# Semaphores of an eight-layer kernel cleared at two seams of six, stores waited for one stage later, and two attention openings reordered

## The chip, the cores and the metric

The kernel runs as one program on 1 core of a Trainium2 chip. Five engines work side by side, each through its own queue in order: TensorE (PE; its weight loads are listed as PEld), VectorE (DVE), ScalarE (ACT), GpSimd (POOL) and SyncE (SP, which here only issues transfers and waits). They meet through semaphores. The metric is the device time of one execution in microseconds, lower is better. The kernel before was timed in three runs: median 1087.17 us, lowest 1084.04, highest 1089.96.

## The reference

x has 2 batches of 1024 tokens of width 256 (2048 rows, 16 tiles of 128 rows); the context has 77 tokens for each batch. Four layer pairs are added to x in turn, each on a layer-normed copy:

```
x = x + attn0(ln(x), ctx, mask)      # 16 heads of 16, biases bq bk bv bo
x = x + ffn0(ln(x))                  # 8 experts, the two best, softmax gates
x = x + attn1(ln(x), ctx, mask)      # 16 heads of 16, bias bo only
x = x + ffn1(ln(x))                  # int8-rounded product with a 256x256 matrix
x = x + attn2(ln(x), ctx, mask)      # one head, context as keys and values
x = x + ffn2(ln(x))                  # 8 experts, two of them in groups, silu
x = x + attn3(ln(x), ctx)            # 16 heads of 64, rotary, relative position bias
x = x + ffn3(ln(x))                  # 8 experts of capacity 320, an overflow path

attn: softmax((q Wq + bq)(k Wk + bk)^T / sqrt(16), masked) (v Wv + bv) Wo + bo
ln:   (x - mean) / sqrt(var + 1e-5)
```

## The kernel before

x stays on chip as 16 tiles. The program is a row of seven stages, in this order: the load stage (`load_stage`), attention 0 (`attn16` with n = 0), the first experts (`moe0`), attention 1 (`attn16` with n = 1), the middle stage (`middle`: ffn1, attn2 and ffn2), the fourth attention (`attn_gqa`), and the last experts (`moe3`).

**Seams.** `run_stage` (L113) runs one stage. Each stage is one block of instructions per engine, and a block ends with a barrier: every engine drains, POOL collects them and releases all. These instructions carry the line of the stage's `with nc.Block()` (L181, L329, L729, L997, L1860). Behind it `run_stage` clears and frees the stage's semaphores (L120, a drain and one range clear on POOL) and sets a second barrier (L121). This is done after every stage but the last, six times.

**The stages' semaphores.** `sem` (L101) allocates one and puts it on the stage's list. By the code the lists have 14 in the load stage, 31 in each `attn16`, 30 in `moe0`, 85 in `middle` and 28 in `attn_gqa`. Semaphores that outlive a stage are allocated in `build` (L2690 to L2706) and never cleared.

**moe0 and the bias stores.** Beside the experts' products (L867, TensorE, and L779 and L782, VectorE) the stage prepares the position bias of the fourth attention: ScalarE loads it by tiles, POOL adds the mask (L852), and ScalarE issues 16 stores, one for each tile, 616 KB each, to DRAM (L829), the last when the last tile is nearly done. The stores count on two semaphores, `masked_out`. SyncE issues the loads of attention 1, the masks and nine large fills of DRAM, and at its end waits until all 16 stores have landed (L750). The fourth attention, two stages on, reads them back.

**The opening of attn16.** Ahead of the loop over 16 tiles:
- TensorE: keys (L489) and values (L495) of the context; then `value_blocks` (L504), 20 records of 128x128 that spread the values over blocks, which waits for VectorE's copy of V (`v_raw`); then for tile 0 `lnT`, two transposes of the normalised rows (L513), and `queries` (L520); then `lnT` of tile 1; then the loop, whose first step is the scores (L529, L535).
- VectorE: mean and variance of all 16 tiles (L146 to L154), the wait for TensorE's values and V's copy with its bias (L369, or L372 without), then the wait for ScalarE's square root and the reciprocal (L374), the masked keys (L378, which TensorE awaits ahead of the scores), the masked copies of the value blocks (L388, six), and in the loop the row maximum (L396), the shift (L402), sum (L414) and reciprocal (L417).
- POOL: the wait for the reciprocal, three tiles of normalisation (L336), three output biases (L341), and in the loop the scaling of the probabilities (L345).
- ScalarE: the square root (L166), two copies of the keys (L427), the copy of the transposed rows (L435) and of the queries (L442, or L445 without bias), and in the loop the exponentials (L457).

The value blocks use banks 4 to 6 of PSUM, the transposes and queries bank 7, the scores banks 0 to 3.

Of the kernel before, what the change touches and what calls it, by code (L numbers as in the profile page):

```python
# [19 lines left out]
NT = T // P  # L20
# [80 lines left out]
def sem(c, name):  # L101

    c.stage_sems.append(c.nc.alloc_semaphore(name=name))
    return c.stage_sems[-1]
# [5 lines left out]
        c.nc.tensor.matmul(bank[:, :], c.identb[:, :], c.RQ[:, :, :].rearrange("p k n -> p (k n)"), start=True, stop=True)  # L110


def run_stage(c, stage, last=False):  # L113


    with ExitStack() as c.stage_ctx:
        c.stage_sems = []
        stage()
    if not last:
        c.nc.clear_and_free_semaphores(c.stage_sems)  # L120
        c.nc.all_engine_barrier()  # L121


def xt(c, i):
# [176 lines left out]
def attn16(c, n, has_bias, scale, n_in):  # L301


    nc = c.nc
# [22 lines left out]
    heads = lambda ap: ap.rearrange("p (h k) -> p h k", k=SK)  # L327

    with nc.Block() as block:  # L329
        @block.gpsimd  # L330
        def _(pool):
            pool.wait_ge(rstd_ok, 1)

            def layer_norm(i, b):
                wait(pool, lnT_ps, i - 1)
                nc.gpsimd.tensor_scalar(c.ln[b][:, :], xt(c, i), mean_of(c, i), rstd_of(c, i),  # L336
                                        ALU.subtract, ALU.mult).then_inc(ln_ok, 1)

            def output_bias(i):
                pool.wait_ge(ln_ok, i + 1)  # L340
                nc.gpsimd.tensor_tensor(xt(c, i), xt(c, i), c.bo[:, :], ALU.add).then_inc(biased, 1)  # L341

            def normalise(i, b):
                pool.wait_ge(rd_ok, i + 1)
                nc.gpsimd.tensor_tensor(heads(c.prob[b]), heads(c.prob[b]),  # L345
                                        rden[b][:, :].unsqueeze(2).to_broadcast([P, H, SK]),
                                        ALU.mult).then_inc(norm_ok, 1)
            layer_norm(0, 0)
            layer_norm(1, 1)
            layer_norm(2, 0)  # L350
            pool.wait_ge(w_in, 16 * n_in)
            for i in range(3):
                output_bias(i)
            for t in range(NT):
                normalise(t, t % 2)
                if inside(t + 4 - 1):
                    layer_norm(t + 3, (t + 3) % 2)
                    output_bias(t + 3)

        @block.vector  # L360
        def _(dve):
            chain = Chain(dve, chain_s)
            nv = nc.vector
            dve_variance(c, chain, ve_ok)
            dve.wait_ge(w_in, 16 * n_in)
            dve.wait_ge(v_ps, 1)
            src = bank_v[0:SK, :].rearrange("k (b n) -> k b n", b=B)
            if has_bias:
                nv.tensor_tensor(V[:, :, :], src, c.bv[0:SK, :].unsqueeze(1).to_broadcast([SK, B, D]),  # L369
                                 ALU.add).then_inc(v_raw, 1)  # L370
            else:
                nv.tensor_copy(V[:, :, :], src).then_inc(v_raw, 1)  # L372
            dve.wait_ge(std_ok, 1)
            nv.reciprocal(c.rstd[:, :], c.std[:, :]).then_inc(rstd_ok, 1)  # L374
            dve.wait_ge(k_sb, 2)
            for k in range(KC):
                for b in range(B):
                    last = nv.tensor_tensor(KB[:, k, b, :, :],  # L378
                                            KT[:, k, b * SK:(b + 1) * SK].unsqueeze(1).to_broadcast([P, HPR, SK]),
                                            c.hmask[:, :].unsqueeze(2).to_broadcast([P, HPR, SK]), ALU.mult)  # L380
            last.then_inc(kb_ok, 1)
            for q in range(3):
                dve.wait_ge(vb_ps, q + 1)
                j0, j1 = q * VPART, min((q + 1) * VPART, NBLK)
                src = bank_vb[q][:, 0:(j1 - j0) * B * VHEADS * HD].rearrange("p (j b g e) -> p j b g e", b=B, g=VHEADS, e=HD)
                sel = vsel[:, j0 * VHEADS:j1 * VHEADS].rearrange("p (j g) -> p j g", g=VHEADS)
                for b in range(B):
                    last = nv.tensor_tensor(VB[:, b, j0:j1, :].rearrange("p j (g e) -> p j g e", e=HD), src[:, :, b],  # L388
                                            sel.unsqueeze(3).to_broadcast([P, j1 - j0, VHEADS, HD]), ALU.mult)
                last.then_inc(v_sb, 1)  # L390

            def step(t, b):

                if inside(t):
                    dve.wait_ge(s_ps, t + 1)
                    nv.reduce_max(c.mx[:, :].rearrange("p (r h) -> p r h", r=GROUPS),  # L396
                                  sview.rearrange("p r (h k) -> p r h k", k=SK), AX).then_inc(mx_ok, 1)
                    wait(dve, pT_ps, (t - 1) * PG)
                    dve.wait_ge(mx_ok, t + 1)
                    for u, done in ((0, shiftA), (1, shiftB)):  # L400
                        r = slice(2 * u, 2 * u + 2)
                        nv.tensor_tensor(c.prob[b].rearrange("p (r h k) -> p r h k", r=GROUPS, k=SK)[:, r],  # L402
                                         sview[:, r].rearrange("p r (h k) -> p r h k", k=SK),
                                         c.mx[:, :].rearrange("p (r h) -> p r h", r=GROUPS)[:, r].unsqueeze(3)
                                         .to_broadcast([P, 2, HPB4, SK]), ALU.subtract).then_inc(done, 1)
                if inside(t - 2):
                    dve.wait_ge(y_ps, t - 1)
                    dve.wait_ge(biased, t - 1)
                    nv.tensor_tensor(xt(c, t - 2), xt(c, t - 2), bank_y[:, 0:D], ALU.add).then_inc(y_used, 1)
                    dve.wait_ge(y_used, t - 1)  # L410
                    nv.bn_stats(bst_of(c, t - 2), xt(c, t - 2))
                if inside(t):
                    dve.wait_ge(exp_ok, t * 2 + 2)
                    nv.reduce_sum(c.den[:, :], heads(c.prob[b]), AX).then_inc(den_ok, 1)  # L414
                    dve.wait_ge(den_ok, t + 1)
                    wait(dve, norm_ok, t - 1)
                    nv.reciprocal(rden[b][:, :], c.den[:, :]).then_inc(rd_ok, 1)  # L417
            pipeline(dve, step, 0, 4, NT - 2, NT + 2)
# [64 lines left out]
        def _(pe):  # L483
# [15 lines left out]
            def value_blocks():  # L499

                pe.wait_ge(v_raw, 1)
                for j, h0 in enumerate(VHEAD0):
                    key0, o = j * P % SK, j % VPART * B * VHEADS * HD
                    last = nt.matmul(bank_vb[j // VPART][:, o:o + B * VHEADS * HD], c.tiled_f[:, key0:key0 + P],  # L504
                                     V[:, :, h0 * HD:(h0 + VHEADS) * HD], start=True, stop=True)
                    if j % VPART == VPART - 1 or j == NBLK - 1:
                        last.then_inc(vb_ps, 1)
# [60 lines left out]
                                     start=(k == 0), stop=(k == KC - 1))  # L568
                last.then_inc(y_ps, 1)

            value_blocks()
            lnT(0, 0)
            queries(0, 0)
            lnT(1, 1)
            pe.wait_ge(kb_ok, 1)

# [134 lines left out]
def moe0(c, d):  # L711

    nc = c.nc
# [8 lines left out]
    rel = [sb(c, f"m0_rel{j}", [P, HB, SK]) for j in range(2)]  # L722
    masked = [sb(c, f"m0_masked{j}", [P, HB, SK]) for j in range(2)]
    rel_in = [sem(c, f"m0_rel_in{j}") for j in range(2)]
    masked_out = [sem(c, f"m0_masked_out{j}") for j in range(2)]
    row_in, row_ok, masked_ok = sem(c, "m0_row_in"), sem(c, "m0_row_ok"), sem(c, "m0_masked_ok")
    gates = g8(c.gates)
    mraw2 = c.prob_pair[1][0:SK, 0:B * S].bitcast(I32)
    with nc.Block() as block:  # L729
        @block.sync  # L730
        def _(sp):
# [14 lines left out]
            for j in range(8):  # L746
                sp.dma_start(c.xd2[j * part * P:(j + 1) * part * P, :].rearrange("(p r) n -> p r n", r=part),
                             c.hole[:, :].unsqueeze(1).to_broadcast([P, part, XW])).then_inc(c.holes, 16)
            for b in range(2):
                sp.wait_ge(masked_out[b], 16 * (NT // 2))  # L750

        @block.vector
        def _(dve):
# [1913 lines left out]
def build(nc, d):  # L2667
    c = Core()
    with ExitStack() as ctx:
# [34 lines left out]
        c.maskT2 = sb(c, "maskT2", [SK, B * S], BF16)  # L2704
        c.hole = sb(c, "hole", [P, XW])
        c.holes = nc.alloc_semaphore(name="holes")  # L2706
        c.xd2 = nc.dram_tensor("routed_rows", (XROWS, XW), F32, kind="Internal").ap()
        c.yd2 = nc.dram_tensor("routed_results", (2 * T, D), F32, kind="Internal").ap()
        c.mb_dram = nc.dram_tensor("masked_bias", (NT * P, H * SK), F32, kind="Internal").ap()
# [15 lines left out]
        c.psall_t = ctx.enter_context(nc.psum_tensor("psum", [P, 8 * 512], F32))  # L2725
        c.psall = c.psall_t[:, :]
        c.ps = [c.psall[:, k * 512:(k + 1) * 512] for k in range(8)]
        run_stage(c, lambda: load_stage(c, d))
        run_stage(c, lambda: attn16(c, 0, True, HD ** -0.5, N_ATTN0))
        run_stage(c, lambda: moe0(c, d))  # L2730
        run_stage(c, lambda: attn16(c, 1, False, HD ** -0.5, N_ATTN0 + N_ATTN1))
        with ExitStack() as both:
            c.stage_ctx = both
            gqa_tiles(c)
            run_stage(c, lambda: middle(c, d))
            run_stage(c, lambda: attn_gqa(c, d))
        run_stage(c, lambda: moe3(c, d), True)


def host_arrays(inputs):  # L2740
# [81 lines left out]
```

## Time and profile before

| what | value |
|---|---|
| three runs, median (lowest to highest) | 1087.17 us (1084.04 to 1089.96) |
| the profiled execution | 1097.08 us, span 1095.2 us, 17120 instructions |
| TensorE busy | 900.1 us, 82% |
| VectorE busy | 742.6 us, 68% |
| ScalarE busy | 374.7 us, 34% |
| POOL busy | 383.3 us, 35% |
| mean granted TensorE clock | 0.919 |

The span reaches from the first to the last instruction, the profiled execution's time also holds what lies around it. Busy shares are averages over seven stages with different limits. In the views below a time is in us from the span's start; a name like POOLq or PEldq is an engine's instruction queue, where barriers, semaphore waits and drains run, which don't count as busy. In brackets stands how long an engine stood idle ahead of an instruction and what ended it. PEclk is the granted clock of TensorE as a share of full speed.

### The profile page before, as it was taken

What the parts mean: (1) busy time and instruction counts of PE and PEld (TensorE: products, weight loads), DVE (VectorE), ACT (ScalarE), POOL (GpSimd) and SP (SyncE); (2) the same over time, 40 slices, a digit from 0 to 9 for tenths busy, and PEclk for the clock granted to TensorE, in tenths of its full rate; (3) what the DMA queues carried; (4) which work ended last, traced back from release to release, by engine and by line L of the source; (5) the groups of instructions that cost most, each with busy time, mean ns of one, the idle gap of its engine ahead of it and who ended that gap; (6) DMA issues with size and microseconds to landing.
All of it is one profiled execution on the core that took longest, in us unless ns stands there. A gap on an engine that the chain in (4) does not pass through costs nothing. (4 is left out here: it accounts for less than half of the span.)

```text
span 1095.2 us, 17120 instructions
## 1 busy us (share of the span) xinstructions
PE 900.1 (82%) x5710; PEld 645.2 (59%) x5711; DVE 742.6 (68%) x1716; ACT 374.7 (34%) x851; POOL 383.3 (35%) x283
## 2 busy tenths in 40 slices
PE   3799979999789966846699379999999509999987
PEld 2677744444467755623388147777776407777777
DVE  5688858978578869767577379999886523243133
ACT  2466540000146547730355123334332302222212
POOL 0576503333356634236155223333333050111111
PEclk9899989999889997957799679999999858999989
DMA  5000079999200008012554541111110563524200
GB/s 167 1 1 0 1 225 296 298 320 324 98 1 1 0 6 248 1 49 93 159 150 139 179 143 47 47 49 58 56 47 1 185 235 111 182 97 148 86 11 18
DMA packets 87225, 117.14 MB, mean 107 GB/s; under 512 B 12432, under 2 KB 75917, under 8 KB 86749
## 3 DMA queue, kind: packets, MB, share of 16 engines
q1 hardware_dynamic: 74871, 85.62, 25.9%
q10 hardware_dynamic: 6960, 17.98, 5.0%
q0 software_dynamic: 5328, 12.70, 3.3%
q8 instruction: 37, 0.61, 0.2%
q14 instruction: 29, 0.24, 0.1%
HBM read 68.08 MB, written 50.16 MB: 108 GB/s over the span
## 5 line engine op out<-in xcount | busy, mean ns | idle before, releaser
L867 PE MATMUL psum<-m_W,lnT 128*128 128x512 f32 x256 | 114.2, 598 | 0.8 <-DVE acc L779 0.8
L345 POOL TENSOR_TENSOR prob<-prob,a_rden 128x1232 f32<-128x1232 f32 x32 | 72.0, 2250 | 81.8 <-DVE a_rden L417 81.8
L867 PEld LDWEIGHTS psum<-m_W,lnT 128*128 128x128 f32 x256 | 47.2, 190 | 59.1 <-issue 56.2
L2124 PE MATMUL psum<-g_VW,pT 128*128 128x256 f32 (+1 forms) x320 | 73.4, 384 | 1.6 <-ACT pT L2045 1.6
L2601 PE MATMUL psum<-x_xT,x_w 128*128 128x320 f32 x256 | 73.1, 445 | 1.5 <-DVE x_xT L2408 1.5
L852 POOL TENSOR_TENSOR m_masked<-m_rel,m_mrow 128x1232 f32<-128x1232 f32 x16 | 41.9, 2620 | 79.6 <-DMA masked_bias<-m_masked 62.3
L2279 POOL DMA_INDIRECT out_x<-x_yt,x_X x20 | 19.7, 986 | 141.3 <-DVE x_yt L2422 140.7
L2124 PEld LDWEIGHTS psum<-g_VW,pT 128*128 128x128 f32 (+1 forms) x320 | 59.5, 190 | 12.6 <-ACT pT L2045 5.1
L1884 POOL TENSOR_TENSOR g_qr<-g_t 128x1024 f32<-128x1024 f32 x16 | 37.9, 2371 | 80.0 <-DVE g_t L1952 80.0
L1887 POOL TENSOR_TENSOR prob<-prob,g_rden 128x1232 f32<-128x1232 f32 x16 | 36.0, 2250 | 83.9 <-DVE g_rden L1982 83.9
L2601 PEld LDWEIGHTS psum<-x_xT,x_w 128*128 128x128 f32 x256 | 49.8, 196 | 23.3 <-issue 4.8
L2079 PE MATMUL psum<-g_Wq,lnT 128*128 128x512 f32 x128 | 62.5, 634 | 0.5 <-ACT lnT L2025 0.5
L396 DVE TENSOR_REDUCE mx<-psum 128x16 f32<-128x1232 f32 x32 | 45.6, 1424 | 22.1 <-PE psum L535 22.0
L2508 ACT ACTIVATE prob<-psum,x_b 128x320 f32<-128x320 f32 x64 | 33.6, 527 | 72.7 <-PE psum L2601 72.1
L2614 PE MATMUL psum<-x_w,prob 128*128 128x256 f32 x256 | 56.6, 379 | 0.0
L1072 POOL DMA_INDIRECT routed_results<-pT,m_idx x39 | 38.4, 985 | 49.5 <-issue 25.0
L336 POOL TENSOR_SCALAR ln<-x_tiles,mean,rstd 128x256 f32<-128x256 f32 x32 | 40.0, 1250 | 37.7 <-DVE rstd L374 37.7
L2614 PEld LDWEIGHTS psum<-x_w,prob 128*128 128x128 f32 x256 | 48.1, 190 | 6.4
L402 DVE TENSOR_TENSOR prob<-psum,mx 128x616 f32<-128x616 f32 x64 | 48.2, 794 | 3.5 <-DVE mx L396 0.5
L414 DVE TENSOR_REDUCE den<-prob 128x16 f32<-128x1232 f32 x32 | 45.7, 1428 | 4.4 <-ACT prob L457 4.1
L463 ACT ACTIVATE pT<-psum 128x512 f32<-128x512 f32 (+1 forms) x96 | 43.6, 527 | 14.4 <-PE psum L550 14.4
L782 DVE SCALAR_TENSOR_TENSOR acc<-psum,gates,acc 128x256 f32<-128x256 f32 x96 | 40.5, 476 | 11.2 <-PE psum L867 11.1
(444 smaller groups left out, 2063.9 us busy)
## 6 DMA issues: line engine op xcount, KB each, us to landing
routed_rows<-hole SPq DMA_DIRECT2D x8, 2210.0 KB, 36.1
masked_bias<-m_masked ACTq DMA_DIRECT2D x16, 616.0 KB, 7.5
g_bias<-masked_bias SPq DMA_DIRECT2D x16, 616.0 KB, 3.7
x_w<-in_L_ffn_w SPq DMA_DIRECT2D x16, 512.0 KB, 4.5
x_w<-in_L_ffn_w SPq DMA_DIRECT2D x8, 1024.0 KB, 5.6
m_xb<-routed_rows SPq DMA_DIRECT2D x39, 130.0 KB, 2.1
m_rel<-in_rel_bias ACTq DMA_DIRECT2D x8, 616.0 KB, 10.7
expert_rows<-hole SPq DMA_DIRECT2D x1, 4680.0 KB, 35.6
```

Of the source, the lines that this page charges most:

```text
L345: nc.gpsimd.tensor_tensor(heads(c.prob[b]), heads(c.prob[b]), rden[b][:, :].unsqueeze(2).to_broadcast([P, H, SK]), ALU.mult).then_inc(norm ...
L396: nv.reduce_max(c.mx[:, :].rearrange("p (r h) -> p r h", r=GROUPS), sview.rearrange("p r (h k) -> p r h k", k=SK), AX).then_inc(mx_ok, 1)
L402: nv.tensor_tensor(c.prob[b].rearrange("p (r h k) -> p r h k", r=GROUPS, k=SK)[:, r], sview[:, r].rearrange("p r (h k) -> p r h k", k=SK), ...
L414: nv.reduce_sum(c.den[:, :], heads(c.prob[b]), AX).then_inc(den_ok, 1)
L463: na.activation(c.pT[b][:, j0 * P:j1 * P], bank_pT[g][:, 0:(j1 - j0) * P], ACT.Copy).then_inc(pT_ok, 1)
L782: ins = nv.scalar_tensor_tensor(out=c.acc[o][:, :], in0=src, scalar=gate, in1=c.acc[o][:, :], op0=ALU.mult, op1=ALU.add)
L852: nc.gpsimd.tensor_tensor(masked[i % 2][:, :, :], rel[i // 2 % 2][:, :, :], mrow[:, i % 2, :].unsqueeze(1).to_broadcast([P, HB, SK]), ALU. ...
L867: last = nt.matmul(c.ps[p][:, :], c.lnT[b][:, k * P:(k + 1) * P], W[:, k, p * 512:(p + 1) * 512], start=(k == 0), stop=(k == KC - 1))
L2079: last = nt.matmul(c.ps[3 + u][:, :], c.lnT[b][:, k * P:(k + 1) * P], Wq[:, k, u * 512:(u + 1) * 512], start=(k == 0), stop=(k == KC - 1))
L2124: last = nt.matmul(bank_y[:, 0:D], c.pT[b][0:w, j * P:(j + 1) * P], VW[0:w, b, j, :], start=(j == 0), stop=(j == NB - 1))
L2601: last = nt.matmul(c.ps[2 + m % 4][:, 0:CAP], w1[b][:, k, m * P:(m + 1) * P], xT[b][:, k, :], start=(k == 0), stop=(k == KC - 1))
L2614: last = nt.matmul(c.ps[6 + ch % 2][:, 0:D], hT[b][:, m, r * P:(r + 1) * P], w2[b][:, m, :], start=(m == 0), stop=(m == MH - 1))
```

## The change

- `run_stage` only runs a stage. Clearing, freeing and the second barrier are now in `free_semaphores`, called twice: after attention 1 (it clears the semaphores of the first four stages at once) and after the fourth attention (those of `middle` and `attn_gqa`). The barrier at the end of each block stays everywhere.
- `masked_out` is allocated in `build` and is on no stage's list. SyncE's wait for the 16 stores moves from the end of `moe0` to attention 1, whose SyncE queue was empty.
- In both `attn16` VectorE takes the reciprocal ahead of the values, and TensorE does the transposes and queries of tile 0 ahead of the value blocks.

```diff
-def run_stage(c, stage, last=False):
-
+def run_stage(c, stage):
 
     with ExitStack() as c.stage_ctx:
-        c.stage_sems = []
         stage()
-    if not last:
-        c.nc.clear_and_free_semaphores(c.stage_sems)
-        c.nc.all_engine_barrier()
+
+
+def free_semaphores(c):
+
+    c.nc.clear_and_free_semaphores(c.stage_sems)
+    c.stage_sems = []
+    c.nc.all_engine_barrier()
...
     with nc.Block() as block:
+        @block.sync
+        def _(sp):
+            if n == 1:
+                for b in range(2):
+                    sp.wait_ge(c.masked_out[b], 16 * (NT // 2))
+
...
             dve_variance(c, chain, ve_ok)
+            dve.wait_ge(std_ok, 1)
+            nv.reciprocal(c.rstd[:, :], c.std[:, :]).then_inc(rstd_ok, 1)
             dve.wait_ge(w_in, 16 * n_in)
             dve.wait_ge(v_ps, 1)
...
-            dve.wait_ge(std_ok, 1)
-            nv.reciprocal(c.rstd[:, :], c.std[:, :]).then_inc(rstd_ok, 1)
             dve.wait_ge(k_sb, 2)
...
-            value_blocks()
             lnT(0, 0)
             queries(0, 0)
+            value_blocks()
             lnT(1, 1)
             pe.wait_ge(kb_ok, 1)
...
-    masked_out = [sem(c, f"m0_masked_out{j}") for j in range(2)]
+    masked_out = c.masked_out
...
-            for b in range(2):
-                sp.wait_ge(masked_out[b], 16 * (NT // 2))
...
+        c.masked_out = [nc.alloc_semaphore(name=f"masked_out{j}") for j in range(2)]
...
+        c.stage_sems = []
         run_stage(c, lambda: load_stage(c, d))
         run_stage(c, lambda: attn16(c, 0, True, HD ** -0.5, N_ATTN0))
         run_stage(c, lambda: moe0(c, d))
         run_stage(c, lambda: attn16(c, 1, False, HD ** -0.5, N_ATTN0 + N_ATTN1))
+        free_semaphores(c)
         with ExitStack() as both:
             c.stage_ctx = both
             gqa_tiles(c)
             run_stage(c, lambda: middle(c, d))
             run_stage(c, lambda: attn_gqa(c, d))
-        run_stage(c, lambda: moe3(c, d), True)
+        free_semaphores(c)
+        run_stage(c, lambda: moe3(c, d))
```

## Rows read from the trace of the kernel before

**Rows 1.** Busy us by engine (instructions), granted clock, DMA share, GB/s of three stretches.

```profile
core 0: us, PE busy (x) PEld busy (x) DVE busy (x) ACT busy (x) POOL busy (x), PEclk, DMA share, GB/s
284.00:290.00 6.00, 3.42 (x11) 2.98 (x12) 1.16 (x7) 1.99 (x4) 0.00 (x0) 0.50 0.01 3
300.00:320.00 20.00, 14.53 (x156) 11.68 (x160) 13.74 (x18) 10.36 (x20) 8.64 (x7) 0.83 0.00 1
340.00:360.00 20.00, 18.94 (x244) 15.53 (x243) 17.61 (x24) 11.92 (x28) 13.61 (x11) 1.00 0.00 0
```

**Rows 2.** Blocks' ends by line: duration ns min/median/max, first and last start us.

```profile
L329 PEldq EVENT_SEMAPHORE  x2: 51/51/51, 142.1 to 407.8; - x2
...
L729 DVEq DRAIN  x1: 270/270/270, 283.5 to 283.5; - x1
...
L729 SPq DRAIN  x1: 7/7/7, 285.7 to 285.7; - x1
...
L729 PEldq EVENT_SEMAPHORE  x1: 51/51/51, 285.9 to 285.9; - x1
...
L997 PEldq EVENT_SEMAPHORE  x1: 51/51/51, 616.9 to 616.9; - x1
```

**Rows 3.** Releases of the seams' own barrier, 100 to 300 and 500 to 700.

```profile
L121 PEldq EVENT_SEMAPHORE  x2: 51/51/51, 142.7 to 286.5; - x2
...
L121 PEldq EVENT_SEMAPHORE  x1: 51/51/51, 617.9 to 617.9; - x1
```

**Rows 4.** The clears: four seams to 500 us, two behind.

```profile
L120 POOLq EVENT_SEMAPHORE_RANGE_CLEAR  x4: 113/198/199, 19.5 to 407.9; - x4
...
L120 POOLq EVENT_SEMAPHORE_RANGE_CLEAR  x2: 178/338/499, 617.1 to 857.5; - x2
```

**Rows 5.** Timeline (start us, us, instruction), TensorE's first work of attention 0.

```profile
20.15 2.42 PE L489 MATMUL psum<-ctxT,Wall 128*128 128x154 f32 x8 [8.59 <-DMA vsel<-in_c_vsel]
```

**Rows 6.** Timeline, the opening of attention 0.

```profile
21.36 0.22 ACT L166 ACTIVATE std<-var_eps 128x16 f32<-128x16 f32 x1
...
22.36 2.78 PE L495 MATMUL psum<-Wall,ctxT 128*77 128x256 f32 x8
...
25.25 0.69 DVE L369 TENSOR_TENSOR a_V<-psum,bv 77x512 f32<-77x512 f32 x1 [3.93 <-PE psum L495]
...
26.00 2.50 PE L504 MATMUL psum<-a_V,lnk 77*128 77x128 f32 x20 [0.86 <-DVE a_V L369]
...
26.21 4.13 POOL L336 TENSOR_SCALAR ln<-x_tiles,mean,rstd 128x256 f32<-128x256 f32 x3 [24.50 <-DVE rstd L374]
27.19 2.04 DVE L388 TENSOR_TENSOR a_VB<-psum,vsel 128x256 f32<-128x256 f32 x6 [0.22 <-PE psum L504]
...
28.33 0.38 PE L513 MATMUL psum<-ident,ln 128*128 128x128 f32 x2
...
29.19 1.16 PE L520 MATMUL psum<-lnT,Wall 128*128 128x128 f32 x8 [0.47 <-ACT lnT L435]
...
30.38 0.63 ACT L442 ACTIVATE qT<-psum,bq 128x128 f32<-128x128 f32 x2 [1.25 <-PE psum L520]
...
31.15 0.41 PE L513 MATMUL psum<-ident,ln 128*128 128x128 f32 x2 [0.81 <-ACT qT L442]
...
32.89 1.44 DVE L396 TENSOR_REDUCE mx<-psum 128x16 f32<-128x1232 f32 x1 [3.66 <-PE psum L535]
```

**Rows 7.** Timeline, the opening of attention 1.

```profile
286.58 2.39 PE L489 MATMUL psum<-ctxT,Wall 128*128 128x154 f32 x8 [5.28 <-PEq L121]
...
288.77 2.69 PE L495 MATMUL psum<-Wall,ctxT 128*77 128x256 f32 x8
...
298.97 1.44 DVE L396 TENSOR_REDUCE mx<-psum 128x16 f32<-128x1232 f32 x1 [3.41 <-PE psum L535]
```

**Rows 8.** The first expert results: two issues, time to landing, and their first reader.

```profile
L931 SPq DMA_DIRECT2D lnT_all<-routed_results x1: 501/501/501, 612.6 to 612.6; - x1
...
DMA to landing us min/median/max: 4.1/4.6/5.1
...
617.96 1.67 DVE L1903 SCALAR_TENSOR_TENSOR x_tiles<-lnk,g_gate,x_tiles 128x256 f32<-128x256 f32 x4 [10.10 <-PEq L121]
```

## The prediction

> **What bounds the kernel now.** I read four views in this order. First the busy time by stretches, to see who leads where [rows 1]: in the steady part of an attention stage (340 to 360 us) TensorE is busy 18.94 and VectorE 17.61 of 20 us, and right after the stage opens (300 to 320 us) only 14.53 and 13.74. The change touches no instruction of the steady parts. It touches the seams between stages and the first 10 us of two attention stages, where nothing is busy throughout and one chain of waits sets the pace. So the second view is the queue instructions of the seams [rows 2 to 4], the third the transfers that the stages behind a seam need first [rows 5, 8], and the fourth the timeline of the two openings [rows 6, 7]. Every stage ends in a barrier, so a stage that ends t earlier moves everything behind it by t, unless a transfer then ends the wait.
>
> **Part 1, the four seams that go.** A seam is two barriers: that of the block, and then a drain, a clear of the stage's semaphores and a barrier of its own. What goes is the time from the first release to the second. It is 142.1 to 142.7 at the seam behind attention 0, 285.9 to 286.5 behind the experts (0.6 each), and 616.9 to 617.9 behind the middle stage (1.0) [rows 2, 3].
> Whether it is gained depends on what the next stage waits for.
> - Load stage to attention 0: nothing. TensorE's first matmul at 20.15 was ended by the landing of vsel, its last input, not by the barrier [rows 5], and TensorE leads from there (part 3). I take 0; the bound on the other side is a whole seam, 0.6.
> - Attention 0 to experts: VectorE starts at once on statistics that it has. 0.6 gained. SyncE's loads start 0.6 earlier with everything else.
> - Experts to attention 1: all inputs are long there. 0.6 gained.
> - Middle to the fourth attention: VectorE's first instruction, at 617.96, reads both halves of the first expert results. The second was issued at 612.6 and took 5.1 to land, so it is there at 617.7 [rows 8]. The removed 1.0 gives back 617.96 - 617.7, about 0.25; the rest becomes a wait for the transfer. Bounds 0 and 1.0.
> Sum 1.45 us.
>
> **Part 2, the two seams that stay.** They now clear more at once. From the code, the clears cover 14, 31, 30 and 31 semaphores in the first four stages (113 to 199 ns), 85 in the middle stage (499 ns) and 28 in the fourth attention (178 ns) [rows 4]. From 31 to 85 that is 300 ns for 54, or 5.6 ns each. The seam behind attention 1 clears 104 now (two have moved out of the expert stage): 199 + 73 x 5.6 = 604 ns, 0.41 more. The one ahead of the last stage clears 113: 499 + 28 x 5.6 = 655 ns, 0.48 more. The clear stands on POOL ahead of the second barrier, so all engines wait for it. Added 0.89 us. Bounds: 0, if the cost hangs on the number of clears, and 2 x 0.5 more if the program splits each into pieces like the longest one.
>
> **Part 3, the wait for the bias stores.** In the expert stage SyncE waits for the last of 16 stores of masked bias, and drains at 285.7. VectorE, the last to compute, had drained by 283.5 + 0.27 = 283.8; TensorE and ScalarE sooner. The release follows the last drain by about 0.2 us in both cases, so the block is released 285.7 - 283.8 = 1.9 us earlier [rows 2]. The wait is now in attention 1's SyncE queue. Nothing stands behind it in that stage, and SyncE's next work is the middle stage's first load, over 120 us later, when the stores have long landed: it costs nothing. What is late next is VectorE itself. Gain 1.9; bounds 1.5 (stores land earlier in other runs) and 2.5.
>
> **Part 4, the openings of attention 0 and 1.** Before, from the end of the value projection the chain runs over both engines [rows 6]: value projection ends at 22.36 + 2.78 = 25.14; VectorE copies V (L369); value blocks on TensorE (L504) 26.00 to 28.50; transposes (L513) to 28.71; ScalarE's copy, then the queries (L520) 29.19 to 30.35; ScalarE copies them (L442) to 31.01; transposes of tile 1 31.15 to 31.56; scores, and VectorE's first row maximum (L396) at 32.89. That is 7.75 us.
> After, transposes and queries stand ahead of the value blocks. The same pieces give: transposes 0.21 behind the projection (28.71 - 28.50), 0.48 over ScalarE (29.19 - 28.71), queries 1.16, value blocks 2.33 (2.50 less the 0.17 by which the next group, at 28.33, begins ahead of their end), transposes 0.21, and 31.56 to 32.89 again for the scores, 1.33. Sum 5.72: 2.03 us less. What goes is the wait for V's copy (it now runs beside the transposes) and that for the query copy (beside the value blocks).
> This needs the first normalised tile at 25.1. POOL's normalisation waits for the reciprocal, which moves from behind V's copy (25.9) to behind ScalarE's square root (21.36 + 0.22 = 21.6): POOL's three tiles, 4.13 us from 26.21 before, then take from about 22 to 26, the first of them done by 22 + 4.13 / 3 = 23.4, give or take 0.4. Covered by over 1 us. V's copy now waits behind the reciprocal, 3.6 us ahead of its own input. VectorE's masked copies of the value blocks (L388) ended at 27.19 + 2.04 = 29.23, 0.73 behind the blocks; now they end at 29.2 + 0.73 = 29.9 and the row maximum is due at 30.9: 0.9 us of cover.
> Attention 1 is the same code: projection ends at 288.77 + 2.69 = 291.46, first row maximum at 298.97, 7.51 us [rows 7]. Less 5.72, it gains 1.79. From the first row maximum on both stages run as before, moved as a whole.
> Together 3.8 us. Bounds: 0, if the cover on VectorE fails (second rival), and 4.5, if the last 0.2 us links shrink too.
>
> **A rule weighed.** The row: TensorE had stood still for 5.28 us when attention 1 began, and from 284 to 290 its granted clock was 0.50, its lower level, 1.2 GHz [rows 1, 7]. Without seam and store wait that idle time is 5.28 - 2.5 = 2.8 us. The Trainium skill (TensorE: Matmul & The Clock Gate, "What's actually happening") says that the slow clock is the default and activity lifts it, and its section on HAM oscillation that a long enough wait throws the array back, each burst then starting cold. By that rule the shorter wait may keep the clock, which is my first rival; by the row alone the opening stays at the lower level.
>
> **The sum.** -1.45 + 0.89 - 1.9 - 3.8 = -6.3 us. The profiled execution took 1097.1 us (span 1095.2), so its like would take 1090.8. The unprofiled runs have a median of 1087.2, 0.9% below that; the same stages are shorter there by little each, so I take the 6.3 over unchanged: 1080.9 us.
>
> **Rivals.**
> 1. The clock stays up over the opening of attention 1. K and V projections took 2.39 + 2.69 = 5.1 us, some four fifths of it at the lower level [rows 1, 7]; at the full one about 2.1 less. For it: the idle time is halved. Against it: the clock also fell in stretches with shorter pauses (300 to 320, mean 0.83). Gives 1078.8.
> 2. The denser opening is worth nothing: at the lower clock level the value blocks take twice 2.33 us, VectorE's masked copies end behind them and stand ahead of the first row maximum, which is then no earlier than before. For it: the clock is low somewhere in each opening, and only 0.9 us covers the copies. Against it: both L504 groups ran at 2.50 us, the full rate. Gives -6.3 + 3.8 = -2.5, 1084.7.
> 3. Slower: the low stretches of the clock land elsewhere. Place: TensorE's chain in the first 20 us of the stages behind the changed seams. 300 to 320 against 340 to 360 shows the price: VectorE does 13.74 instead of 17.61 us of work, 22% or 4.4 us lost in 20 [rows 1], part of it pipeline fill. It needs more than 6.3 us of new loss, so at least two more such stretches; with three, +13.2 - 6.3 = +6.9, 1094. Against it: shorter idle times make low clock rarer. The spread of the three runs, 1084.0 to 1090.0, says that such shifts are some 3 us either way.
> 4. The clears cost far more than 5.6 ns for each semaphore, or the four removed seams were covered by transfers as at two of them: then parts 1 and 2 give +0.9 to +2 instead of -0.6, total -4 to -5, still no slower. 1082.5.
>
> **How the numbers follow.** The main case 0.55 (own range 1077.5 to 1084.5), rival 1 0.15, rival 2 0.14, rival 3 0.08, rival 4 0.08. Low end of the range: rival 1 less the run spread, 1075. High end: rival 2 plus the run spread, 1087. No change is within 0.5%, 5.4 us, about what a measurement of this kernel can tell. The main case, at 6.3 with 2 to 3 us of spread, is past that in two of three cases: 0.36; rival 1 nearly always: 0.14; rivals 2 and 4 one time in four: 0.05. Faster 0.55, same 0.37, slower 0.08.
>
> **What would show it.** Right: no clear at four seams and two clears near 600 and 650 ns; attention 1 released 0.2 us behind VectorE's drain, and its first matmul some 2.7 us behind TensorE's last one; from the end of the value projection to the first row maximum 5.7 us in both stages; the first matmul of attention 0 still ended by vsel; VectorE's first instruction of the fourth attention waiting for the expert results. Wrong: a row maximum that waits for L388 on its own engine, value blocks that take 4 us or more, clears of over 1 us, or steady parts whose pace differs from 17.61 us of VectorE work in 20.

## The result, and the profile after

The changed kernel takes 1083.37 us (median of 20 runs, 1079.32 to 1089.56), the kernel before, in runs beside it, 1088.62 us (median of 20, 1084.04 to 1093.44). The ratio is 0.9948, with a 95% interval of 0.9935 to 0.9961: 5.7 us less, between 4.2 and 7.1. The forecast was 6.3 less and 1080.9 us. It started from 1087.2; from the 1088.6 that more runs give, the same 6.3 would have made 1082.3.

The two profiled executions lie further apart, 1097.08 and 1083.64 us. That is no size of the change: 1097.08 is above every one of the 20 runs of the kernel before. The totals of the page after, busy us by engine and the granted clock in 40 slices:

```profile
span 1081.8 us, 17068 instructions
PE 894.0 (83%) x5710; PEld 642.5 (59%) x5711; DVE 741.7 (69%) x1716; ACT 374.4 (35%) x851; POOL 385.1 (36%) x283
...
PEclk9899989999889988959799689999999858999989
```

So I compare stages and steps, not spans. In the code after, attention 0 and 1 are at L331, the experts at L737, the middle stage at L1003.

**The openings.** The timeline of attention 0 after (start us, duration, instruction, idle time before it and its releaser), which answers to [rows 5, 6]:

```profile
19.50 2.42 PE L497 MATMUL psum<-ctxT,Wall 128*128 128x154 f32 x8 [8.21 <-DMA vsel<-in_c_vsel]
20.46 0.25 DVE L374 RECIPROCAL rstd<-std 128x16 f32<-128x16 f32 x1 [0.28 <-ACT std L168]
20.82 2.44 POOL L344 TENSOR_SCALAR ln<-x_tiles,mean,rstd 128x256 f32<-128x256 f32 x2 [19.12 <-DVE rstd L374]
21.71 3.12 PE L503 MATMUL psum<-Wall,ctxT 128*77 128x256 f32 x8
24.67 0.38 PE L521 MATMUL psum<-ident,ln 128*128 128x128 f32 x2
24.95 0.69 DVE L379 TENSOR_TENSOR a_V<-psum,bv 77x512 f32<-77x512 f32 x1 [4.24 <-PE psum L503]
25.53 1.16 PE L528 MATMUL psum<-lnT,Wall 128*128 128x128 f32 x8 [0.47 <-ACT lnT L443]
26.52 2.40 PE L512 MATMUL psum<-a_V,lnk 77*128 77x128 f32 x20
27.61 2.05 DVE L396 TENSOR_TENSOR a_VB<-psum,vsel 128x256 f32<-128x256 f32 x6 [1.06 <-PE psum L512]
28.75 0.38 PE L521 MATMUL psum<-ident,ln 128*128 128x128 f32 x2
30.47 1.44 DVE L404 TENSOR_REDUCE mx<-psum 128x16 f32<-128x1232 f32 x1 [0.81 <-PE psum L543]
```

The value projection (L503) ends at 24.83, the first row maximum (L404) begins at 30.47: 5.64 us instead of 7.75. The two waits that went are seen in the middle: transposes (L521) and queries (L528) run while VectorE copies V (L379), and the value blocks (L512) while ScalarE copies the queries. POOL has two normalised tiles by 23.3. The masked copies (L396) end at 29.66, 0.81 us ahead of the row maximum, which waits for the scores and not for them.

Attention 1 after, the answer to [rows 7]:

```profile
279.49 1.73 PE L497 MATMUL psum<-ctxT,Wall 128*128 128x154 f32 x8 [2.74 <-PEq L737]
281.01 3.18 PE L503 MATMUL psum<-Wall,ctxT 128*77 128x256 f32 x8
...
289.82 1.44 DVE L404 TENSOR_REDUCE mx<-psum 128x16 f32<-128x1232 f32 x1 [0.81 <-PE psum L543]
```

281.01 + 3.18 = 284.19 to 289.82 is 5.63 us instead of 7.51. TensorE was idle for 2.74 us ahead of its first matmul, where it had been for 5.28.

**The block of the experts.** Queue instructions (duration in ns, first and last start in us), and the last store of masked bias with its landing, the answer to [rows 2]:

```profile
L737 SPq DRAIN  x1: 371/371/371, 253.3 to 253.3; - x1
...
L737 DVEq DRAIN  x1: 270/270/270, 279.0 to 279.0; - x1
...
L737 ACTq EVENT_SEMAPHORE  x1: 17/17/17, 279.4 to 279.4; - x1
...
L835 ACTq DMA_DIRECT2D masked_bias<-m_masked x1: 326/326/326, 275.0 to 275.0; - x1
DMA to landing us min/median/max: 3.3/3.3/3.3
```

SyncE drains at 253.3 and is out of the way; VectorE's drain, over at 279.3, sets the release. But this execution's last store landed at 275.0 + 3.3 = 278.3: the old wait would have cost it nothing.

**The seams that stay**, both clears and POOL's drains ahead of them, the answer to [rows 4]:

```profile
L121 POOLq EVENT_SEMAPHORE_RANGE_CLEAR  x2: 592/622/651, 398.0 to 844.0; - x2
...
L121 POOLq DRAIN  x2: 214/220/226, 397.8 to 843.8; - x2
```

The clears are 592 and 651 ns (worked out ahead: 604 and 655). The drain ahead of them, 109 ns at the same place before the change (the seam ahead of the last stage), is 226 ns. From release to release these seams now take 1.11 and 1.18 us where they took 0.61 and 0.58.

**The fourth attention**, VectorE's first instruction, the answer to [rows 8]:

```profile
605.49 1.67 DVE L1909 SCALAR_TENSOR_TENSOR x_tiles<-lnk,g_gate,x_tiles 128x256 f32<-128x256 f32 x4 [9.62 <-DMA lnT_all<-routed_results]
```

Its releaser is now the transfer, as forecast. The block was released at 604.87, so it starts 0.62 behind that; before it started 1.09 behind it.

**The pace of the steady part**, the three stretches of [rows 1], each 7.0 to 7.3 us earlier (busy us by engine, granted clock, DMA share, GB/s):

```profile
276.70:282.70 6.00, 3.26 (x13) 2.55 (x13) 3.60 (x15) 1.99 (x4) 1.23 (x2) 0.79 0.11 45
293.00:313.00 20.00, 17.51 (x184) 14.30 (x184) 14.34 (x17) 9.26 (x21) 11.24 (x8) 0.74 0.00 1
333.00:353.00 20.00, 18.72 (x252) 15.20 (x254) 17.50 (x24) 11.85 (x28) 12.75 (x10) 1.00 0.00 0
```

VectorE does 17.50 us of work in 20 in the third, where it did 17.61. Over the opening of attention 1 the granted clock is now 0.79 on average, where it was 0.50: its low stretch is shorter. In the second row it is lower than before, 0.74 instead of 0.83.

### The profile page after: what moved, and what is told of

The parts are those of the page before. It is cut to its first block and busy times, and to the rows that moved or that the text cites. A ratio compares the mean times of both kernels' runs of the same rounds, so it can differ in the third digit from the quotient of the medians.

```text
span 1081.8 us, 17068 instructions
## 1 busy us (share of the span) xinstructions
PE 894.0 (83%) x5710; PEld 642.5 (59%) x5711; DVE 741.7 (69%) x1716; ACT 374.4 (35%) x851; POOL 385.1 (36%) x283
## 5 line engine op out<-in xcount | busy, mean ns | idle before, releaser
L404 DVE TENSOR_REDUCE mx<-psum 128x16 f32<-128x1232 f32 x32 | 45.6, 1425 | 15.4 <-PE psum L543 15.3
L471 ACT ACTIVATE pT<-psum 128x512 f32<-128x512 f32 (+1 forms) x96 | 43.5, 527 | 13.4 <-PE psum L558 13.4
```

The lines of the kernel that those rows point to most:

```text
L471: na.activation(c.pT[b][:, j0 * P:j1 * P], bank_pT[g][:, 0:(j1 - j0) * P], ACT.Copy).then_inc(pT_ok, 1)
```

## The experiments

Lines that begin with + or - are the edit. "To before" is the ratio to the kernel before on the same chip, with its 95% interval.

**The openings alone.** Kernel before, with both edits of the openings:

```
+            dve.wait_ge(std_ok, 1)
+            nv.reciprocal(c.rstd[:, :], c.std[:, :]).then_inc(rstd_ok, 1)
             dve.wait_ge(w_in, 16 * n_in)
             ...
-            dve.wait_ge(std_ok, 1)
-            nv.reciprocal(c.rstd[:, :], c.std[:, :]).then_inc(rstd_ok, 1)
...
-            value_blocks()
             lnT(0, 0)
             queries(0, 0)
+            value_blocks()
```

> Only part 4: reciprocal, transposes and queries ahead in both attentions; six clears and the old place of the store wait stay. Main case: from the end of the value projection to the first row maximum 5.6 to 5.8 us in both attentions (before 7.75 and 7.51), time 3.8 us under the kernel before, some 1083.4 where that has 1087.2. Rival 2 (denser opening worth nothing): the row maximum is held by the masked copies L388, time equal to before within 1 us.

Measured 1085.61 us, 0.9963 to before (0.9946 to 0.9979): 4.0 us less, between 2.3 and 5.9. Both openings take 5.63 us. What the timeline says is gained there, 2.1 + 1.9 = 4.0, agrees with the 4.0 us by which the whole kernel is shorter, although the seams and the store wait of the old kind stand behind it.

**The store wait alone.** The wait moved into attention 1, all six seams kept:

```
     with nc.Block() as block:
+        @block.sync
+        def _(sp):
+            if n == 1:
+                for b in range(2):
+                    sp.wait_ge(c.masked_out[b], 16 * (NT // 2))
...
-            for b in range(2):
-                sp.wait_ge(masked_out[b], 16 * (NT // 2))
```

> Only part 3: the wait for the 16 bias stores stands in attention 1. Main case: the expert stage is released about 0.2 us behind VectorE's drain, 1.9 us earlier, time 1.9 us less. Rival 1 of the clock: TensorE's idle time at the opening of attention 1 falls from 5.3 to 3.4 us and the granted clock may be up for part of the projections, which makes it up to 2.1 us more. A rival of no gain: the stores are taken up by another wait, time as before.

Measured 1089.89 us, 1.0005 to before (0.9986 to 1.0025): no gain is seen, and one of more than 1.5 us is ruled out, the 1.9 of the forecast with it. Its trace says why, VectorE's drain and the last store:

```profile
L735 DVEq DRAIN  x1: 270/270/270, 282.1 to 282.1; - x1
...
L833 ACTq DMA_DIRECT2D masked_bias<-m_masked x1: 326/326/326, 277.6 to 277.6; - x1
DMA to landing us min/median/max: 4.3/4.3/4.3
```

The store landed at 277.6 + 4.3 = 281.9, ahead of VectorE's 282.4. In the profiled execution of the kernel before, on which the 1.9 us rested, the same store took 6.1:

```profile
L829 ACTq DMA_DIRECT2D masked_bias<-m_masked x1: 327/327/327, 279.4 to 279.4; - x1
...
DMA to landing us min/median/max: 6.1/6.1/6.1
```

**The seams alone.** Only the clears and their barriers moved together (the edit of run_stage and free_semaphores in the diff).

> Only parts 1 and 2: clears at two seams of six. Main case: two clears of some 0.6 and 0.65 us, four seams gone of which two give 0.6 each and one 0.25, net 0.6 us less, not to be told from no change. If every removed seam counted in full it would be 2.8 - 0.9 = 1.9 us less; rival 4 (nothing gained at the covered ones and dearer clears): 0 to 1 us more.

Measured 1088.4 us, 0.9989 to before (0.9971 to 1.0008): 1.2 us less, give or take 2. This agrees with the forecast of 0.56 and also with none; the size rests on the rows of the seams. The old store wait is still in this kernel, and here it costs something:

```profile
L731 DVEq DRAIN  x1: 270/270/270, 284.7 to 284.7; - x1
L731 SPq DRAIN  x1: 7/7/7, 285.9 to 285.9; - x1
```

SyncE's drain starts 0.9 us behind the end of VectorE's, at 285.0, and holds the release up by 1.0.

**Openings and store wait together.**

> The change without its seams (parts 3 and 4, six clears stay). Main case: 5.7 us less than before, the full change within 0.6 us of it. If the parts share something (the clock at the opening of attention 1), it differs from the sum of the two alone.

Measured 1086.65 us, 0.9963 to before (0.9942 to 0.9983): 4.0 us less, between 1.9 and 6.3. The middle value is that of the openings alone, so nothing is seen of the store wait; the interval is too wide to exclude the 5.7 that the forecast makes of the two together.

**The two halves of the opening, each alone.** First the reciprocal ahead of V's copy, without the new order on TensorE:

> The kernel before with only VectorE's reciprocal ahead of the values, TensorE's order as before. Theory: POOL's first tile was not what TensorE waited for (the value blocks ended after it), so the opening stays at 7.7 and 7.5 us and the time is that of before. Also one more sample of the last bias store against VectorE's drain: if it lands 0 to 0.5 us behind the drain, part 3 of the prediction took an unusual execution for the rule; if 1.5 to 2 us, the trace of before was typical.

Measured 1093.57 us beside 1092.45 of before, 1.0007 (0.9984 to 1.0029). The openings take 7.75 and 7.51 as before: POOL's tiles are early and nobody needs them. Then TensorE's order alone, the reciprocal left behind V's copy:

```
-            value_blocks()
             lnT(0, 0)
             queries(0, 0)
+            value_blocks()
```

> The kernel before with only TensorE's order changed, reciprocal still behind V's copy. Theory: the first transposes wait for POOL's first tile (about 1.7 us behind the reciprocal, 2.8 us behind the projection's end), and the value blocks now stand behind them: 8.6 us instead of 7.7 from the projection to the first row maximum in both attentions, 2 us slower than before. If the two edits were independent halves of 3.8 us, this would be 1 to 2 us faster.

Measured 1103.29 us, 1.0090 to before (1.0057 to 1.0124): 9.8 us slower, where I expected some 2. Timeline of its attention 0:

```profile
21.63 2.53 PE L495 MATMUL psum<-Wall,ctxT 128*77 128x256 f32 x8
...
26.98 0.69 PE L513 MATMUL psum<-ident,ln 128*128 128x128 f32 x2 [2.83 <-POOL ln L336]
...
28.14 2.07 PE L520 MATMUL psum<-lnT,Wall 128*128 128x128 f32 x8 [0.47 <-ACT lnT L435]
...
30.01 4.47 PE L504 MATMUL psum<-a_V,lnk 77*128 77x128 f32 x20
...
33.67 1.34 DVE L388 TENSOR_TENSOR a_VB<-psum,vsel 128x256 f32<-128x256 f32 x4 [0.95 <-PE psum L504]
...
37.35 1.44 DVE L396 TENSOR_REDUCE mx<-psum 128x16 f32<-128x1232 f32 x1 [2.34 <-PE psum L535]
```

TensorE now asks first for the normalised tile, and that still waits for V's copy and the reciprocal: it stands still for 2.83 us. That pause is the smaller part. Behind it each group takes nearly twice as long (value blocks 4.47 instead of 2.50, queries 2.07 instead of 1.16). The opening takes 37.35 - 24.16 = 13.2 us, 5.4 more than before, and that of attention 1 takes 12.92, again 5.4 more. Two times 5.4 is 10.8, which lies within the interval of the measured 9.8 (6.2 to 13.5). The granted clock of two stretches (columns as above):

```profile
24.00:34.00 10.00, 6.70 (x30) 6.14 (x30) 2.80 (x9) 1.01 (x3) 6.18 (x6) 0.62 0.00 1
34.00:44.00 10.00, 9.19 (x59) 6.74 (x58) 5.25 (x8) 3.88 (x7) 0.00 (x0) 0.50 0.01 2
```

and of the changed kernel in the first of them:

```profile
24.00:34.00 10.00, 7.83 (x70) 6.33 (x68) 6.46 (x14) 3.84 (x8) 4.55 (x4) 1.00 0.00 1
```

A clock of 0.50, that is 1.2 GHz, holds from 34 to 44 us although TensorE is then busy for 9.19 of 10 us. The Trainium skill (TensorE: Matmul & The Clock Gate, "HAM oscillation — how this bites in real kernels") says that a wait, if it is long enough, throws the array back to the slow clock and the next burst starts in it; this trace agrees, for the clock is at 1.00 until 26 us, falls within the pause of 2.83 us, and is at 0.50 from 27 us on, where the transposes begin. The price here, 5.4 us in each opening, is larger than the wait itself. So the two halves do not add: 0, +9.8, and together -4.0.

**The gates behind the seams.** The changed kernel, with vsel awaited by VectorE (its reader) instead of TensorE, and the second half of the first expert results on a semaphore of its own:

```
-        ...d["c_vsel"]).then_inc(c.w_in, 16)
+        ...d["c_vsel"]).then_inc(c.vsel_in, 16)
-N_ATTN0, N_ATTN1 = 9, 5
+N_ATTN0, N_ATTN1 = 8, 5
+            dve.wait_ge(c.vsel_in, 16)
             for q in range(3):
...
-                     ).then_inc(c.back_in[k], 16)
+                     ).then_inc(c.back_two if k == 0 and o == 1 else c.back_in[k], 16)
...
+                    if tiles[-1] < 4 and o == 1:
+                        dve.wait_ge(c.back_two, 16)
```

> The full change, and the two transfers that still hold a stage behind a removed seam get semaphores of their own: vsel is awaited by VectorE ahead of the masked value copies, not by TensorE and VectorE at the stage's start, and the second half of the first expert results ahead of its own sums. Theory: attention 0 starts TensorE 0.6 to 0.7 us earlier, the fourth attention VectorE 0.5 to 0.7 us earlier, 1.2 us under the full change. Rival: x's statistics or the first half of the results gate then, and nothing is gained.

Measured 1084.06 us, 0.9931 to before (0.9908 to 0.9955), which is not to be told from the 0.9948 and 0.9942 of the changed kernel. TensorE's first work and VectorE's in the fourth attention:

```profile
19.52 2.42 PE L498 MATMUL psum<-ctxT,Wall 128*128 128x154 f32 x8 [8.33 <-DMA bv<-in_L_xattn_bv]
...
607.27 1.67 DVE L1912 SCALAR_TENSOR_TENSOR x_tiles<-lnk,g_gate,x_tiles 128x256 f32<-128x256 f32 x4 [9.29 <-PEq L1004]
```

TensorE starts no earlier than in the changed kernel (19.50). With vsel out of the way it waits for the bias bv, which lands 0.1 us ahead of vsel: a gate taken away leaves the next one. That bv stands so close is special to this edit. It took 5.5 to 5.7 us from issue to landing in the three kernels that have the edit and 3.4 to 5.2 in the eleven others; in the changed kernel it landed at 13.75 + 4.8 = 18.6. The cause stays open. In the fourth attention the first instruction follows the release, at 607.17, by 0.10 instead of 0.62 us.

**The changed kernel once more**, on the chip of the three kernels below.

> The full change again, timed beside the three below, and one more execution profiled. Expected: 5 to 6 us under the kernel before; from the projection to the first row maximum 5.63 us in both attentions as in all earlier runs with the reordered opening; the last bias store lands ahead of VectorE's drain, so that the moved wait saves little in this execution.

Measured 1086.72 us, 0.9942 to before (0.9921 to 0.9962): 6.3 us less, a little more than expected. The openings take 5.63 and 5.62 us. The last store landed at 275.0 + 4.2 = 279.2, 0.1 us behind the end of VectorE's drain, where I had expected it ahead.

**A warm clock over the seam.** The changed kernel with 12 products into an unused bank at the end of the expert stage:

```
                 step(i, i % 2)
+            keep_warm(c, c.ps[5], 12)
```

> The full change with 12 products into an unused bank at the end of the expert stage on TensorE (results unused), so that TensorE is busy up to the barrier. Theory of the clock: the opening of attention 1 then runs wholly at the upper level, and from the first key product to the end of the value projection it takes 3.7 to 4.0 us instead of 4.7 to 4.9: 0.7 to 1 us less than the full change. Rival: the products delay TensorE's drain past VectorE's, or the clock falls anyway a few us later in the stage, and nothing is gained.

Measured 1086.08 us, 0.9938 to before (0.9916 to 0.9960); the changed kernel has 0.9942 to 0.9948, so nothing is seen of the expected 0.7 to 1 us. Timeline of its opening of attention 1:

```profile
283.48 1.29 PE L497 MATMUL psum<-ctxT,Wall 128*128 128x154 f32 x8 [0.30 <-PEq L737]
284.60 1.89 PE L503 MATMUL psum<-Wall,ctxT 128*77 128x256 f32 x8
...
286.74 0.44 PE L521 MATMUL psum<-ident,ln 128*128 128x128 f32 x2 [0.25 <-POOL ln L344]
...
292.59 1.44 DVE L404 TENSOR_REDUCE mx<-psum 128x16 f32<-128x1232 f32 x1 [0.81 <-PE psum L543]
```

The projections take 3.01 us instead of 4.70, and 0.47 of that goes at once to a wait for POOL's first tile (6.10 us from their end to the row maximum instead of 5.63). Another part goes to the seam: TensorE's own drain, with the added products in it, now ends last, at 283.2, and holds the release up by 0.25 us (VectorE stands idle for 0.56 us over this seam instead of 0.31).

**The clock behind the first row maximum.** The two gates of above, and 14 products in the second step of the loop of attention 0 and 1, ahead of the next transposes. The wait for `v_sb` moves ahead with them:

```
+                if is_static(t) and t == 1:
+                    pe.wait_ge(v_sb, 3)
+                    keep_warm(c, c.ps[4], 14)
                 if inside(t + 2):
                     lnT(t + 2, b)
                 if inside(t - 1):
-                    if is_static(t) and t == 1:
-                        pe.wait_ge(v_sb, 3)
```

> The full change, the two transfers on semaphores of their own, and 14 products into a free bank on TensorE in tile 1 of both attentions, where it waits for POOL (results unused). Theory of the clock: the low stretch in tile 1 to 2 goes, the step from the second to the third row maximum takes some 7 us instead of 7.9 to 8.9 in both stages, 2 to 3 us under the variant with two gates alone. Rival: that step hangs on POOL's scaling and third normalisation, which no clock shortens: under 0.5 us.

Measured 1081.65 us, 0.9911 to before (0.9883 to 0.9939). The two gates alone have 0.9931 (0.9908 to 0.9955), so the time does not show the share of the products. In attention 0 the step from the second to the third row maximum takes 6.92 us instead of 7.88 to 8.93; in attention 1 it stays at 8.76. In both the clock is at 0.50 when the products begin. In attention 0 they begin at 37.61 and the clock is back at 1.00 from 38 us on; in attention 1 they begin at 295.27 and it stays at 0.50 until 297 (0.92 from 297 to 299). Why it rose sooner in the one than in the other is not shown. The same with 10 products at the seam as well:

> As the one before, and 10 products at the end of the expert stage. Theory: the projection of attention 1 takes 3.0 us as with 12 products, but its first row maximum comes 6.1 us behind it because POOL's first tile is then awaited; net 1.1 us less, and TensorE's drain no longer behind VectorE's. Rival: it costs more in other executions than it brings, same time as without it.

Measured 1081.79 us, 0.9898 to before (0.9876 to 0.9921), the steps 6.86 and 7.10. This is the lowest ratio of all; the changed kernel on the same chip has 0.9942 (0.9921 to 0.9962), so the intervals just touch. That it beats the change is likely, but how much of this is due to the gates and how much to the products cannot be told from these times, nor whether the seam's products add to it.

The trace of the kernel with 14 products also holds the dearest case for the old store wait:

```profile
L739 DVEq DRAIN  x1: 270/270/270, 276.7 to 276.7; - x1
...
L837 ACTq DMA_DIRECT2D masked_bias<-m_masked x1: 326/326/326, 273.2 to 273.2; - x1
DMA to landing us min/median/max: 6.5/6.5/6.5
```

Landed at 279.7, 2.7 us behind the end of VectorE's drain at 277.0.

**The price of a clear.** The changed kernel with 40 semaphores more in the clear behind attention 1, 144 instead of 104:

```
+        for j in range(40):
+            sem(c, f"spare{j}")
         free_semaphores(c)
```

> The full change with 40 more semaphores, never used, in the clear behind attention 1 (144 instead of 104). At 5.6 ns each the clear takes 592 + 224 = 816 ns; if a clear had a fixed cost or went by pieces, 592 ns or a jump of 0.5 us.

One run, 1090.57 us, which says nothing at this size. Its clears and drains:

```profile
L121 POOLq EVENT_SEMAPHORE_RANGE_CLEAR  x2: 651/730/809, 401.2 to 851.0; - x2
...
L121 POOLq DRAIN  x2: 226/250/273, 400.9 to 850.7; - x2
```

592 ns became 809, so 5.4 ns each, and the drain ahead of it grew by 59 ns though POOL did the same work.

## Why the prediction was right, and where it was not

**The openings (forecast -3.8): right.** 5.64 and 5.63 us where 5.72 was worked out, 4.0 less together; alone they give 4.0 (2.3 to 5.9). The half-and-half kernels show that the forecast's condition, the first normalised tile at 25.1, was the heart of it. Its absence costs not the 2 to 3 us of the wait but 5.4 us in each stage.

**The store wait (forecast -1.9): the mis-sized term.** The step "VectorE drained by 283.8, SyncE at 285.7" was read rightly, but from an execution in which the last store took 6.1 us. Alone, the edit gives nothing (0.9986 to 1.0025). In the profiled executions of all fourteen kernels that last landing stands between 1.5 us ahead of the end of VectorE's drain and 2.7 behind it (in the one with the seams alone it is not recorded, and I take it from SyncE's drain). It holds the release up in five of them, or would with the wait in its old place (before, openings alone, seams alone, the change again, 14 products), by 2.0, 0.4, 1.0, 0.4 and 2.9 us, the landing's distance and some 0.2 more for SyncE: 0.5 us as a mean over fourteen. The bounds of 1.5 and 2.5 left zero out, and they should not have: "stores land earlier in other runs" was written down as 0.4 us of play, when the transfer's own time varies by 3.6 us (2.9 to 6.5 from issue to landing).

**The seams that go (forecast -1.45): right in kind.** Attention 0 to experts: VectorE starts at 138.71, 0.10 behind the release, 0.63 gained. Experts to attention 1: 0.60. Load to attention 0: still gated by vsel. Middle to the fourth attention: 0.47 instead of 0.25, again because a transfer is taken at the size that one execution shows.

**The seams that stay (forecast +0.89): +1.10.** The clears were right to 12 ns; POOL's drain ahead of them, some 0.1 us longer at each, was missed.

**The balance.** -4.0 - 0.5 - 0.63 - 0.60 - 0.47 + 1.10 = -5.1 us, and -5.5 with 0.4 us in the last tiles of attention 1 that I cannot explain (below). Measured -5.7, -4.2 to -7.1. By these rows the store wait was 1.4 too large and the openings and seams together 0.2 to 0.6 too small. The total came out within 0.6 us of the forecast in part by luck: some of the 1.4 was made up by the other terms, and the rest by what these rows do not explain.

**The rivals.** The first, a clock that stays up over attention 1's opening, came half true and was worth little. With 2.74 us of idle time instead of 5.28 the first matmuls take 1.73 instead of 2.39, but the projections together, 4.70 instead of 4.88, gained only 0.2: the clock still fell while they ran. This stretch shows it (columns as above):

```profile
280.00:284.00 4.00, 4.00 (x14) 2.83 (x14) 0.97 (x6) 1.44 (x4) 2.43 (x2) 0.57 0.00 0
```

The prize was judged about rightly: with 12 products ahead of the seam the projections took 3.01 us, 1.9 less than before, where the rival had 2.1.

The second, VectorE's copies ahead of the row maximum, did not happen: 0.81 us of cover, even behind a slow projection. The third, low stretches that land elsewhere, did not show as a loss, but its price did: it is what the kernel with TensorE's order alone paid. The fourth was wrong in both halves: a clear costs 5.4 to 5.6 ns for each semaphore, and three of the four seams gave something.

**The profiled pair.** 13.4 us lie between the two spans and 5.7 between the kernels. From the release behind attention 1 to that behind the middle stage it is 1.9 us less after, with no edit in the work between them and a seam there that is 0.5 longer; the stages with edits are shorter by more than the edits give. In the fourteen profiled executions this same stretch takes between 204.4 and 211.2 us, so one execution of each kernel says nothing of a change of this size. To take the 6.3 over onto the median unchanged was right; to take a term from that execution's transfers was not.

## What to carry to other kernels

Two edits of one chain are one edit: move a consumer ahead only after its producer is moved, since here a pause of 2.8 us on TensorE cost 5.4 us with the slow clock behind it. A wait for a transfer is worth what its landing takes over many executions, not in one: look at the same transfer's landings in the rest of the profile, and let the lower bound reach zero when their spread is as large as the gain. When a gate is removed, look for the one that then ends the wait: here it stood 0.1 us from the old one.

## What the runs showed of the hardware that was not expected

- The length of an opening, from the end of the value projection to the first row maximum, hangs almost alone on the instruction order. With the old order it is 7.75 to 7.76 us in attention 0 and 7.50 to 7.51 in attention 1. With the new one it is 5.62 to 5.64 in fourteen openings of eighteen. Two with products at the seam have 6.10, where POOL is awaited, and two have 5.84 and 5.85 (attention 0 with 12 products, attention 1 with 40 more semaphores), where the first transposes, right behind a projection of 3.62 us, took 0.63 us instead of 0.38.
- A clear takes 5.4 to 5.6 ns for each semaphore from 31 to 144 of them, and the drain on POOL ahead of it grows with the size of the clear (109 to 226 ns at one place, 107 to 214 and 273 at the other).
- The slow clock can long outlast a pause: in the kernel with TensorE's order alone 2.83 us of idle time were followed by 0.50, 1.2 GHz, from 27 us on; it still held from 34 to 44 us, with TensorE busy for 9.19 of these 10 us.
- From the last row maximum of attention 1 to its release seven of the eight kernels with two clears take 14.1 us (the eighth, in a stretch of low clock, 15.4), all six kernels with the six old clears 14.5. The place is VectorE's shift behind the row maximum, before and after:

```profile
395.22 1.50 DVE L402 TENSOR_TENSOR prob<-psum,mx 128x616 f32<-128x616 f32 x2 [0.51 <-DVE mx L396]
```

```profile
385.16 1.50 DVE L410 TENSOR_TENSOR prob<-psum,mx 128x616 f32<-128x616 f32 x2
```

VectorE waits 0.51 us for its own row maximum in the one and not in the other, with the same instructions. The cause stays open; no run here takes the numbers of the semaphores apart from the count of the clears.
